# The MLP's output layer in a fused transformer kernel, with its operands exchanged for batches 0 to 6

## The reference, cut to what matters

```python
def _tlin(x, w, s):
    return jnp.einsum('bsi,oi->bso', x, w) * s
h = jax.nn.silu(_tlin(x, w1_w, w1_s)) * _tlin(x, w2_w, w2_s)      # 128 -> 512
h = jax.nn.gelu(_tlin(h, h1_w, h1_s), approximate=False)          # 512 -> 512
h = jax.nn.gelu(_tlin(h, h2_w, h2_s), approximate=False)          # 512 -> 512
return _tlin(h, w3_w, w3_s)                                       # 512 -> 128
...
x = _layernorm(x + _L1_ffn_ref(x, ...), axis=-1)
```

## Time and profile before

| | us |
|---|---|
| median of three runs | 382.56 (380.55 to 382.93) |
| the profiled execution | 381.66 |
| its span, first to last instruction | 379.9 |

### The profile page before, as it was taken

How to read it: one execution, slowest core, us unless ns; L and a number is a source line. 1 busy time by engine, 2 the same in 40 slices (tenths; PEclk the granted TensorE clock), 3 DMA queues, 4 the chain that set the end, 5 groups by cost and what they waited for, 6 DMA issues and landing times.

```text
span 379.9 us, 8516 instructions
## 1 busy us (share of the span) xinstructions
PE 331.9 (87%) x2540; PEld 304.5 (80%) x2540; DVE 261.9 (69%) x853; ACT 210.8 (55%) x430; POOL 178.4 (47%) x238
## 2 busy tenths in 40 slices
PE   3799889977875999999975999999977999999990
PEld 1788778866855998898975888888767999999990
DVE  3558886974772568768874689987785776667741
ACT  2266556734431455454547778886547667667340
POOL 0014577663464345886578667644133342243200
PEclk9899999996697999999999999999999999999997
DMA  8980001121132523322501200000000000000001
GB/s 275 428 338 1 16 29 39 35 59 27 42 88 63 183 85 114 110 63 57 156 22 46 88 0 2 3 3 0 2 3 1 2 14 16 14 14 1 14 16 31
DMA packets 17033, 23.71 MB, mean 62 GB/s; under 512 B 3424, under 2 KB 14176, under 8 KB 16208
## 3 DMA queue, kind: packets, MB, share of 16 engines
q1 hardware_dynamic: 13712, 17.97, 14.4%
q0 software_dynamic: 2272, 4.69, 3.7%
q10 hardware_dynamic: 1008, 0.53, 0.5%
HBM read 17.45 MB, written 6.73 MB: 64 GB/s over the span
## 4 chain that ended last, share of the span: by engine, by line
PE 65%; DVE 7%; issue 5%; ACT 3%; POOL 3%; another core or an unknown queue 2%; DVEq 0%; POOLq 0%; ACTq 0%
PE ps L1945 9%; PE ps L1946 9%; PE ps L1582 8%; PE ps L1583 6%; PE ps L1584 6%; PE ps L1782 5%; PE ps L1890 4%; PE ps L1997 3%; PE ps L1771 3%; PE ps L1905 2%; PE ps L1665 1%; ACT sb_stage L734 1%; PE ps L1917 1%; PE ps L1747 1%
## 5 line engine op out<-in xcount | busy, mean ns | idle before, releaser
L1945 PE MATMUL ps<-sb_w_hi,sb_fh_hi 128*128 128x256 f32 x256 | 63.2, 287 | 3.9 <-POOL sb_w_lo L605 2.3
L1946 PE MATMUL ps<-sb_w_lo,sb_fh_hi 128*128 128x256 f32 x256 | 62.1, 283 | 0.0
L1945 PEld LDWEIGHTS ps<-sb_w_hi,sb_fh_hi 128*128 128x128 f32 x256 | 49.0, 192 | 5.0 <-POOL sb_w_lo L605 2.8
L1946 PEld LDWEIGHTS ps<-sb_w_lo,sb_fh_hi 128*128 128x128 f32 x256 | 49.0, 192 | 0.0
L605 POOL TENSOR_TENSOR sb_w_lo<-sb_x_in,sb_w_hi 128x256 fp32r<-128x256 f32 x28 | 21.4, 794 | 44.2 <-DVE sb_w_hi L1523 44.2
L457 POOL DMA_INDIRECT routed<-sb_rows_of,sb_row x32 | 31.8, 993 | 18.2 <-issue 9.0
L1782 PE MATMUL ps<-sb_w,sb_stage 128*128 x234 | 34.4, 285 | 5.0 <-ACT sb_xT_in L740 4.2
L1582 PE MATMUL ps<-sb_w_hi,sb_rT_hi 128*128 x78 | 30.9, 396 | 6.5 <-issue 4.4
L1782 PEld LDWEIGHTS ps<-sb_w,sb_stage 128*128 128x128 f32 x234 | 30.4, 198 | 5.7 <-issue 5.6
L556 POOL DMA_INDIRECT answers<-sb_stage x24 | 25.0, 1043 | 12.4 <-issue 7.8
L577 POOL TENSOR_TENSOR sb_w_lo<-sb_x_in,sb_w_hi 128x512 fp32r<-128x512 f32 x16 | 20.7, 1293 | 19.9 <-DVE sb_w_hi L1389 19.8
(11 more groups left out here) (304 smaller groups left out, 1039.8 us busy)
## 6 DMA issues: line engine op xcount, KB each, us to landing
sb_stage<-in_w SPq DMA_DIRECT2D x2, 1408.0 KB, 13.0
sb_stage<-routed SPq DMA_DIRECT2D x24, 65.0 KB
sb_w<-in_w SPq DMA_DIRECT2D x1, 1536.0 KB, 17.4
sb_x_in<-in_x_tok SPq DMA_DIRECT2D x1, 1024.0 KB, 8.8
sb_x_in<-in_ff_h SPq DMA_DIRECT2D x1, 1024.0 KB
sb_xT_in<-in_ff_h SPq DMA_DIRECT2D x1, 1024.0 KB
sb_got_first<-answers SPq DMA_DIRECT2D x4, 256.0 KB, 3.4
sb_w<-answers SPq DMA_DIRECT2D x4, 256.0 KB, 3.5
```

Source lines behind the costliest of these rows:

```text
L1945: mm(dst, w_hi, x_hi, start=start, stop=False)
L1946: last = mm(dst, w_hi, x_lo, start=False, stop=stop and exact)
```

## The change

For batches 0 to 6 the output layer is turned round. The unscaled weights stand, in high and low parts, and the high and low parts of `f_last` move: 8 matmuls of 128x256 in the exact branch, 12 in the other. The result has features on partitions, so ScalarE copies it out of PSUM with the scale (`output_rows` on ScalarE), and TensorE transposes it back with two transposes (`output_turns`), after the third layer's second tile. VectorE makes the high parts l_hi (`high_last`, four casts per batch) and GpSimd the low parts l_lo (`low_last`, four subtractions per batch). Batch 7 keeps the old form. The weights are split by GpSimd in the expert stage (`split_ff_out`), two copies follow in the attention stage, VectorE tests the two low parts, and the semaphores of some weight parts are merged.

```diff
+        fo_hi = [over(w, 2 * FF, 2, D) for w in (front_hi, front_lo)]
+        fo_less = [w[:, :].rearrange("p (k d) -> p k d", d=D) for w in (mid, x1T)]
+        fo_lo = over(w13_lo, TOKENS + 3 * FF_TILES * SEQ, FF_TILES, D)
...
+        l_hi, l_lo = (over(w, TOKENS + 2 * FF_TILES * SEQ, FF_TILES, SEQ) for w in (w13_hi, w13_lo))
+        f_outT = work[:, 3, SEQ:]
...
+
+            def split_ff_out():
+                pool.wait_ge(g0["logits"], BATCHES)
+                pool.wait_ge(g0["out"], BATCHES)
+                for n in range(2):
+                    nc.gpsimd.tensor_copy(fo_hi[n], ff_out[:, 2 * n:2 * n + 2, :]).then_inc(wt["ff_out"], 1)
+                for n in range(2):
+                    pool.wait_ge(wt["ff_out"], n + 2)
+                    nc.gpsimd.tensor_tensor(fo_less[n], ff_out[:, 2 * n:2 * n + 2, :], fo_hi[n].bitcast(fp32),
+                                            ALU.subtract).then_inc(wt["ff_out"], 1)
...
-                elif n < 14:
-                    split_bout(n - 7)
+                elif n == 7:
+                    split_ff_out()
+                elif n < 15:
+                    split_bout(n - 8)
...
+            def low_last(b, tiles):
+                for m in tiles:
+                    if live(b, BATCHES - 1):
+                        pool.wait_ge(ff["l_hi"], FF_TILES * b + m + 1)
+                        nc.gpsimd.tensor_tensor(l_lo[:, m, :], f_last[:, m, :], l_hi[:, m, :].bitcast(fp32), ALU.subtract).then_inc(ff["l_lo"], 1)
+
+            def output_root(b):
+                if live(b, BATCHES):
+                    inverse_root(ff["mv"], ff["rstd"], b + 1, mv, veps, rstd, TILES)
+
             def mlp_rest(i):
-                b = i - 3
-                if live(b, BATCHES):
-                    inverse_root(ff["mv"], ff["rstd"], b + 1, mv, veps, rstd, TILES)
+                output_root(i - 3)
+                low_last(i - 2, range(FF_TILES))
...
+                pool.wait_ge(mo["up"], SLOT_TILES)
+                for n in range(2):
+                    pool.wait_ge(wt["ff_out"], n + 4)
+                    nc.gpsimd.tensor_copy(fo_lo[:, 2 * n:2 * n + 2, :], fo_less[n]).then_inc(wt["ff_out"], 1)
...
-            steps(pool, BATCHES, MLP_LAG, mlp_rest, ahead=1, first=EARLY)
+            steps(pool, BATCHES, MLP_LAG, mlp_rest, ahead=1, first=EARLY, left=2)
+            output_root(6)
+            output_root(7)
...
-                        wait(act, ff["out_mm"], b)
+                        wait(act, ff["l_lo"], FF_TILES * (b - 1) + m + 1)
...
+            def output_rows(b):
+                if live(b, BATCHES - 1):
+                    act.wait_ge(ff["out_mm"], b + 1)
+                    wait(act, ff["out_tr"], b)
+                    nc.scalar.activation(f_outT, ps[:, 0, 0:SEQ], ACT.Copy, scale=ff_s[:, 4, 0:1]).then_inc(ff["outT"], 1)
...
-                mlp_first(i)
+                mlp_first(i, range(FF_TILES - 1))
+                output_rows(i - 3)
+                mlp_first(i, (FF_TILES - 1,))
...
+            output_rows(5)
             third_gelu(6, (0, 1))
             second_gelu(7, (0, 1))
             second_gelu(7, (2, 3))
             third_gelu(6, (2, 3))
-            third_gelu(7, range(FF_TILES))
+            third_gelu(7, (0, 1))
+            output_rows(6)
+            third_gelu(7, (2, 3))
...
+                if t in (34, 35):
+                    dve.wait_ge(wt["ff_out"], t - 30)
+                    odd_part(2 * FF_TILES + 1 + t - 34, fo_less[t - 34].rearrange("p k d -> p (k d)"))
...
-            def mlp_rest(i):
-                b = i - 3
-                if live(b, BATCHES):
-                    dve.wait_ge(ff["out_mm"], b + 1)
+            def output_rows(b):
+                if live(b, BATCHES):
+                    if isinstance(b, int) and b == BATCHES - 1:
+                        dve.wait_ge(ff["out_mm"], BATCHES)
+                        rows = ps[:, 0:TILES, 0:D]
+                    else:
+                        dve.wait_ge(ff["out_tr"], b + 1)
+                        rows = by_tile(ps[:, 0, SEQ:])
                     wait(dve, ff["out"], b)
-                    out_rows = ps[:, 0:TILES, 0:D] if isinstance(b, int) and b == BATCHES - 1 else by_tile(ps[:, 0, 0:TILES * D])
-                    V.tensor_tensor(by_tile(f_res), out_rows, x_kept[:, b, :, :], ALU.add).then_inc(ff["res"], 1)
+                    V.tensor_tensor(by_tile(f_res), rows, x_kept[:, b, :, :], ALU.add).then_inc(ff["res"], 1)
                     dve.wait_ge(ff["res"], b + 1)
                     moments(f_res, stats, mv, TILES, D, ff["mv"], b + 1)
+
+            def output_norm(b):
+                if live(b, BATCHES):
                     dve.wait_ge(ff["rstd"], 2 * b + 2)
                     wait(dve, ff["stored"], 16 * b)
                     normalise(f_out, f_res, mv, rstd, TILES, D, ff["out"])
+
+            def high_last(b, tiles):
+                for m in tiles:
+                    if live(b, BATCHES - 1):
+                        dve.wait_ge(ff["g2"], FF_TILES * b + m + 1)
+                        wait(dve, ff["out_mm"], b)
+                        V.tensor_copy(l_hi[:, m, :], f_last[:, m, :]).then_inc(ff["l_hi"], 1)
+
+            def mlp_rest(i):
+                output_rows(i - 3)
+                high_last(i - 2, (0, 1))
+                output_norm(i - 3)
+                high_last(i - 2, (2, 3))
                 low_parts_of_second(i - 1)
                 high_parts_of_first(i)
...
-            steps(dve, BATCHES, MLP_LAG, mlp_step, ahead=1, first=EARLY)
+            steps(dve, BATCHES, MLP_LAG, mlp_step, ahead=1, first=EARLY, left=3)
+            output_rows(5)
+            high_last(6, (0, 1))
+            low_parts_of_second(7, (0, 1))
+            output_norm(5)
+            low_parts_of_second(7, (2, 3))
+            high_last(6, (2, 3))
+            output_rows(6)
+            output_norm(6)
+            output_rows(7)
+            output_norm(7)
...
-            def output_layer(b):
+            def output_layer(b, exact):
+                pe.wait_ge(ff["l_lo"], FF_TILES * (b + 1))
                 wait(pe, ff["res"], b)
-                if isinstance(b, int) and b == BATCHES - 1:
-                    for k in range(FF_TILES):
-                        pe.wait_ge(ff["g2"], FF_TILES * b + k + 1)
-                        for t in range(TILES):
-                            last = mm(ps[:, t, 0:D], f_last[:, k, t * P:(t + 1) * P], ff_out_w[:, k, :],
-                                      start=k == 0, stop=k == FF_TILES - 1)
-                    last.then_inc(ff["out_mm"], 1)
-                    return
-                pe.wait_ge(ff["g2"], FF_TILES * (b + 1))
+                for k in range(FF_TILES):
+                    last = mlp_product(ps[:, 0, 0:SEQ], fo_hi[k // 2][:, k % 2, :], fo_lo[:, k, :], l_hi[:, k, :], l_lo[:, k, :],
+                                       k == 0, k == FF_TILES - 1, exact)
+                last.then_inc(ff["out_mm"], 1)
+
+            def output_turns(b):
+                pe.wait_ge(ff["outT"], b + 1)
                 for t in range(TILES):
-                    for k in range(FF_TILES):
-                        last = mm(ps[:, 0, t * D:(t + 1) * D], f_last[:, k, t * P:(t + 1) * P], ff_out_w[:, k, :],
+                    last = transpose(ps[:, 0, SEQ + t * D:SEQ + (t + 1) * D], f_outT[:, t * P:(t + 1) * P], ident)
+                last.then_inc(ff["out_tr"], 1)
+
+            def last_output_layer():
+                pe.wait_ge(ff["res"], BATCHES - 1)
+                for k in range(FF_TILES):
+                    pe.wait_ge(ff["g2"], FF_TILES * (BATCHES - 1) + k + 1)
+                    for t in range(TILES):
+                        last = mm(ps[:, t, 0:D], f_last[:, k, t * P:(t + 1) * P], ff_out_w[:, k, :],
                                   start=k == 0, stop=k == FF_TILES - 1)
                 last.then_inc(ff["out_mm"], 1)
...
+                pe.wait_ge(wt["ff_out"], 7)
...
-                if live(i - 3, BATCHES):
-                    output_layer(i - 3)
+                output_layer(i - 3, exact)

                 third_layer(i - 2, (0,), exact)
                 if live(i, BATCHES):
                     first_layer(i, (FF_TILES - 1,), exact)
                 third_layer(i - 2, (1,), exact)
+                output_turns(i - 3)
...
-                output_layer(5)
+                output_layer(5, exact)
                 third_layer(6, (0, 1), exact)
+                output_turns(5)
                 second_layer(7, (0, 1), exact)
                 second_layer(7, (2, 3), exact)
                 third_layer(6, (2, 3), exact)
-                third_layer(7, (0,), exact)
-                output_layer(6)
-                third_layer(7, (1, 2, 3), exact)
-                output_layer(7)
+                third_layer(7, (0, 1), exact)
+                output_layer(6, exact)
+                third_layer(7, (2,), exact)
+                output_turns(6)
+                third_layer(7, (3,), exact)
```

(9 more changed lines are left out.)

44 lines of the change are left out of this document (21 added, 23 removed).

## The result

Kernel before 381.56 us (median of 4 runs beside it, 378.21 to 382.93), changed kernel 390.27 us (387.24 to 393.38): ratio 1.0232, 95% interval 1.0181 to 1.0282, so the change costs 7 to 11 us. The prediction said 390.5 us and 384 to 395. The ratio and its interval leave out runs in a slower state of the chip, of the changed kernel the one of 393.38 us. The profiled execution took 387.24 us, the one of before 381.66.

What follows compares the result with a forecast made beforehand. TensorE bound the kernel before; after, VectorE's loop through act 0, held by GpSimd subtractions, would. Four periods +5.2, output layer 4 to 5 +1.8, tail +1.3: +8.3 us, forecast 390.5 us, range 384 to 395.

Steps and rivals of the forecast that it cites:

- TensorE's side, -0.66 a batch: MLP output layer on TensorE: old 1.78 us, new products 0.91 and transposes 0.21, so 0.66 us saved per batch.
- the slack of 0.3: Before the change, VectorE's first product of a batch (act 0) may slip 0.3 us before TensorE's fourth first-layer tile waits.
- Each subtraction on GpSimd costs VectorE about 0.7 us, once: MLP: a GpSimd subtraction meeting a VectorE cast, subtraction or normalisation holds VectorE about 0.7 us, once.
- The walk: VectorE's operations timed from one batch's residual add to the next; act 0 done at 10.7 us, next add at 12.6.
- The loop closes at 12.6: MLP batch period, through VectorE and act 0: 12.6 us against 11.27, +1.3 us per batch.
- The stalls: TensorE's two waits per batch: 0.6 us at the third layer's first tile, 1.3 at the first layer's fourth.
- Output layer 4 to 5, +1.8: MLP: output layer 5 waits for its batch's last l_lo, 11.7 us behind output layer 4 instead of 9.9, +1.8.
- Tail, +1.3: End of the MLP: two cheaper output layers, -1.3, against waits of 1.5, 0.5 and 0.6; +1.3 us.
- Four periods, +5.2: MLP from output layer 0 to output layer 4: four longer batch periods, +5.2 us.
- Expert stage at 0: Ahead of the MLP: GpSimd's 2.1 us of casts and subtractions for the weight split taken as 0, at most +2.
- The rival in which VectorE keeps the port: MLP: VectorE's back-to-back operations pass ahead of GpSimd's; +0.5 us per batch, period 13.1, total +11.2, 393.8 us; chance 0.14.

Runs made afterwards that it cites:

- e3_tensor_only: Changed kernel with only TensorE's and ScalarE's part: third GELU writes the high parts, no new VectorE casts or GpSimd subtractions; ratio 1.0078 to the kernel before.
- s_subs: Kernel before plus the split of the output weights and one GpSimd subtraction per third-GELU tile, old output layer kept; ratio 1.0057 to the kernel before.
- s_weights: Kernel before with only the split of the output weights and VectorE's reductions of their low parts; ratio 1.0009 to the kernel before.
- e5_copy: Changed kernel, l_hi copied by ScalarE, l_lo subtracted on VectorE, VectorE's list reordered, first layer's fourth tile after third layer's second; ratio 1.0061 to the kernel before.

## Why the prediction held, step by step

- *TensorE's side, -0.66 a batch:* right. Eight products at 0.113 and transposes at 0.14 + 0.08 are in the rows above. e3_tensor_only shows that it was never to be had in this order, which is what the slack of 0.3 said.
- *Each subtraction on GpSimd costs VectorE about 0.7 us, once:* the mechanism is right, the price too high. 0.7 is GpSimd's step; VectorE pays what is left of it when its own operation arrives, 0.31 to 0.53 us per operation here. The four together cost VectorE 1.71 us in these rows and 1.40 of busy time in s_subs, not 2.8. The walk had priced them by their meeting times, about 2.0, and so came out only 0.2 late. The four l_lo lengthen the two normalisations together by 0.75, the first pair by 0.53 and 0.43, and the casts l_hi by little, since GpSimd waits for the third of them itself (0.36). s_subs shows the same without any new VectorE work. From the add, VectorE reaches the end of the first pair at 6.06 (345.88; forecast 6.25), the casts of the first layer at 8.05 (8.25), and act 0 at 9.96 (10.15).
- *The loop closes at 12.6:* 12.12, 12.45 and 12.47 from output layer to output layer where the clock is full, so 0.1 to 0.5 shorter than forecast. The stalls were to be 0.6 and 1.3; start to start they exceed the normal 0.12 by 0.63 (347.33 to 348.08) and 1.18, and behind each the second matmul starts 0.1 late.
- *Output layer 4 to 5, +1.8:* 346.54 to 358.18 is 11.64 against 9.91, +1.7, released by l_lo as said. *Tail, +1.3:* 21.51 against 20.59, +0.9.
- *Four periods, +5.2:* the term that was off by mechanism: the working kept the clock at its full level. 295.28 to 346.54 is 51.3 against 45.1, +6.2, and it holds one period of 14.22 in which the clock fell (below). Without its 1.8 it would be +4.4. Two errors of opposite sign, 0.8 and 1.8 us, so the total agrees better than its terms, and that is luck. So is part of the agreement of 390.5 with 390.27: single runs of the changed kernel lie between 387.24 and 393.38.
- *Expert stage at 0:* not contradicted; the interval of s_weights allows up to 2 us.
- *The rival in which VectorE keeps the port* is refuted: GpSimd's subtractions in pairs take 1.44 and 1.61, 0.70 and 0.83 from start to start, while VectorE issues back to back. Beside L619 the long rows of VectorE and GpSimd's come in turn. The lock that the Trainium skill describes ("SBUF — State Buffer", section on the two separate sides) agrees with each of the rows above; a trace doesn't show what it is that the engines share.
- *Where I was most wrong* is in what the experiments' totals would be: s_subs +2.6 where the working gave +4.0, e5_copy -0.3 where it gave -1.7. Both times the period was within 0.3 us, and five or more of them add up.

## What to carry to other kernels

Moving work off a full engine pays only as far as the next loop has room: find the instruction that the full engine will wait for once it is early, and read its slack first (here 0.3 us, where 0.66 was to be saved). Price an instruction on GpSimd by what it does to VectorE's SBUF operations beside it, here 0.3 to 0.5 us for each one that meets one, and not by GpSimd's free time; 1.4 us more on VectorE itself was cheaper here than four subtractions on an engine that was busy a third of the time. Side work that fits alone may not fit together: 0.2 and 0.3 us became 1.1.
